# A two-layer graph network kernel: the bfloat16 split of layer two's rows moves into layer one's store

## The chip, the cores and the metric

The kernel runs on one NeuronCore of a Trainium2 chip. The metric is the time of one execution on the device in microseconds; the lower, the better. The profile is of one execution of the same program under the hardware profiler.

## The reference

50,000 nodes with 64 features each and 100,000 edges, sorted by destination (25,000 random ones, the same turned round, and one loop for each node). Two graph convolutions, a residual and a layer norm:

```
def _ngcf_conv(x, W1, W2, src, dst, n_nodes):
    deg_out = clip(segment_sum(ones, src), 1); deg_in = clip(segment_sum(ones, dst), 1)
    norm = rsqrt(deg_out[src] * deg_in[dst])
    msg = (x[src] @ W1 + x[src] * x[dst] @ W2) * norm[:, None]
    return x @ W1 + segment_sum(msg, dst)

h = relu(_ngcf_conv(x, W1_1, W2_1, src, dst, n))
h = _ngcf_conv(h, W1_2, W2_2, src, dst, n)
return _layernorm(x + h)              # float32, over the 64 features, eps 1e-5
```

## The kernel before

A node's message needs the sum S over its edges of the scaled source rows; then its result is (S + x) W1 + (S * x) W2, S scaled by the node's own factor. The kernel has a preparation (`prepare`: sort positions, degrees, factors, and layer one's table in HBM), layer one and layer two (`layer`, with l = 0 and l = 1), and behind them a general path that this input does not take.

Both layers have the same frame. The edges lie in 398 chunks of 128, gathered eight to a batch (51 batches, the last two of 4 and 2). The destinations are 392 tiles of 128 nodes, eight to a group (50 groups, the last two of 4). Step s of the loop in `STEPS` works on batch s. `ended(s)` names the groups whose last edges lie in batch s; nearly every step has one.

- GpSimd issues one indirect DMA for each chunk (line 799): 128 rows of the layer's table in HBM, one for each partition. In layer one the first 48 come from x itself (line 258). `rows` is a ring of 8 batches in layer one, 4 in layer two. A gather waits only until its slot is free: in layer one until the batch seven or eight back was cut (`rows_scaled`), in layer two until the batch four back was summed (`summed`).
- VectorE makes a batch's selection matrices (`select`, line 1077), one 0/1 matrix of 128 x up to 512 for a chunk.
- TensorE sums (`add_up`, line 828): for each chunk and each of up to four tiles three matmuls, one for each bfloat16 part of the gathered rows, whose sum is the float32 row to within rounding. The sums gather in PSUM (`p_sum`, three banks).
- Then a group goes through `join` (VectorE, adds the node's own row), `scale` (ScalarE), `products` (VectorE, S + x and S * x), `turn` (TensorE), `turned_back` (ScalarE), `multiply` (TensorE, line 853).
- In layer one ScalarE's `relu` makes the hidden rows and writes their first bfloat16 part into `y`; VectorE's `rests` (line 1114) writes what is left in float32 behind it, and SP stores the group to layer two's table (line 772). A row of that table is 384 bytes: 64 bfloat16 numbers and 64 float32 numbers. For the last four groups (`END_GROUPS`) VectorE does both in `end_rows` (lines 1154 and 1157).
- In layer two a group's end is the residual and the layer norm (`centre`, `square`, `vary`, `deviate`, `normalize`).

Where do the three parts come from? In layer one VectorE makes them of the gathered rows in `cut` (lines 1099, 1103, 1107): the scaled row `yr`, what is left behind its upper half, `rest`, and what is left behind that, `lo`. The upper half of a float32 number is read in place as a bfloat16 number, at a stride of two. In layer two the first part lies in the row, the second is the upper half of the float32 rest, and the third is made by VectorE in `last_part` (line 1087), which overwrites the rest's lower halves:

```
def last_part(b):
    left = first_and_rest(rows[:, b % RING, 0:BATCH[b]])[1]
    landed(dve, b)
    V.tensor_tensor(halves(left)[:, :, :, 0], left, halves(left)[:, :, :, 1], ALU.subtract).then_inc(split, 1)
```

`landed` waits for the batch's gathers. TensorE waits for `split` in both layers before it sums a batch.

Each engine works off its instructions in the order of the code. Some steps also make operands for a count of the edges (`hots`, lines 1121 and 1124; every second step of layer one from 8 to 44, three steps in four of layer two up to 41). In steps 0 to 4 of layer one VectorE looks up degrees (`pick`) between the instructions of `cut`. Layer two starts behind a barrier, once layer one's last store has landed.

Of the kernel before, what the change touches and what calls it, by code (L numbers as in the profile page):

```python
# [7 lines left out]
P = 128  # L8
# [583 lines left out]
GN = 8  # L592
# [36 lines left out]
def layer(nc, l, x, out, tables, flag, keepers):  # L629

    k = keepers
    with ExitStack() as ctx:
# [17 lines left out]
        if l == 0:  # L650
            rest, lo = sb("rest", [P, 2, 8, D]), sb("lo", [P, 2, 8, D], BF16)
# [3 lines left out]
            picks = sb("picks", [P, 2, TILES], F16)  # L655
# [4 lines left out]
            yr = sb("yr", [P, 2, 8, D])  # L660
# [17 lines left out]
        hots_made, counted, lanes_read, split = sem("hots_made"), sem("counted"), sem("lanes_read"), sem("split")  # L678
        if l == 0:
            rows_scaled, rest_made, hidden_made = (sem(n) for n in ("rows_scaled", "rest_made", "hidden_made"))  # L680
# [13 lines left out]
        def first_and_rest(a):  # L694

            return a.bitcast(BF16)[:, :, 0:D], a[:, :, D // 2:THREE]

        def halves(a):

            return a.bitcast(BF16).rearrange("p c (d two) -> p c d two", two=2)  # L700

        def parts(b):

            if l == 0:
                return tops(yr[:, b % 2]), tops(rest[:, b % 2]), lo[:, b % 2]
            first, left = first_and_rest(rows[:, b % RING])
            return first, halves(left)[:, :, :, 1], halves(left)[:, :, :, 0]
# [39 lines left out]
        def sync(sp):  # L747
# [14 lines left out]
            def store(g):  # L762
# [5 lines left out]
                if l == 0:  # L768
                    sp.wait_ge(high_made, g + 1)
                stores[g % 4] += 1  # L770
# [31 lines left out]
        def tensor(pe):  # L802
# [13 lines left out]
            def add_up(b):  # L816
                pe.wait_ge(sel_made, b + 1)
                pe.wait_ge(split, b + 1)
                for i in range(BATCH[b]):
# [4 lines left out]
                    for n, t in enumerate(band(c)):  # L824
                        g = GROUP_OF[t]
                        first = c == BEGINS[g] and t == GROUP[g][0]
                        for q, part in enumerate(parts(b)):
                            last = nc.tensor.matmul(p_sum[g % BANKS][:, t - GROUP[g][0], :], sel[:, b % 2, i, n * P:(n + 1) * P], part[:, i],  # L828
                                                    start=first and q == 0, stop=q == 2, skip_group_check=True)
# [12 lines left out]
            def multiply(g):  # L842
                pe.wait_ge(uvt_made, g + 1)
                if g in (g2, g3):
                    pe.wait_ge(uv_made, GROUPS)
                else:
                    done(pe, y_made if l == 0 else centred, g - 1)
# [50 lines left out]
        def scalar(act):  # L898
# [30 lines left out]
            def relu(g):  # L929
# [15 lines left out]
                A(first_and_rest(y[:, g % 4, 0:w])[0], from_rows, ACT.Copy).then_inc(high_made, 1)  # L945
# [31 lines left out]
            for s in STEPS:  # L977
# [11 lines left out]
                if l == 0:  # L989
                    for g in ended(s - 2):  # L990
                        relu(g)
# [42 lines left out]
        def vector(dve):  # L1034
# [48 lines left out]
            def last_part(b):  # L1083

                left = first_and_rest(rows[:, b % RING, 0:BATCH[b]])[1]
                landed(dve, b)
                V.tensor_tensor(halves(left)[:, :, :, 0], left, halves(left)[:, :, :, 1], ALU.subtract).then_inc(split, 1)  # L1087

            def cut(b):

                n, j = BATCH[b], b % 2
# [7 lines left out]
                V.tensor_tensor(yr[:, j, 0:n], rows[:, b % RING, 0:n, 0:D], rows[:, b % RING, 0:n, D:ROW].to_broadcast([P, n, D]), ALU.mult).then_inc(rows_scaled, 1)  # L1099
                pick_next(1)  # L1100
                dve.wait_ge(rows_scaled, b + 1)
                high = yr[:, j, 0:n].rearrange("p c d -> p (c d)")
                V.tensor_tensor(rest[:, j, 0:n].rearrange("p c d -> p (c d)"), high, top(high), ALU.subtract).then_inc(rest_made, 1)
                pick_next(2)
                dve.wait_ge(rest_made, b + 1)
                low = rest[:, j, 0:n].rearrange("p c d -> p (c d)")
                V.tensor_tensor(lo[:, j, 0:n].rearrange("p c d -> p (c d)"), low, top(low), ALU.subtract).then_inc(split, 1)
                pick_next(3)

            def rests(g):  # L1110

                dve.wait_ge(high_made, g + 1)
# [638 lines left out]
```

## Time and profile before

| | |
|---|---|
| time, median of 3 runs (lowest to highest) | 1152.91 us (1151.71 to 1153.17) |
| profiled execution, first to last instruction | 1700.1 us |
| busy in the profiled execution: TensorE, its weight loads | 1004.6 us, 885.6 us |
| VectorE | 998.9 us |
| ScalarE | 728.1 us |
| GpSimd | 831.9 us |
| mean granted TensorE clock | 0.727 |

The profiled execution has no other time of its own than this span, and the span is 547 us longer than a run. The profile's times of single instructions and their order can be read; its stretches can't be laid on a run's time as they stand. In the rows below a line gives the start in us from the first instruction, the duration in us, engine, line of the kernel, operation, what it writes and reads, the number of like instructions, and in square brackets how long the engine had been idle before it and what ended that. Instructions of one engine overlap by some 0.1 us, so that the distance from start to start is what one costs its engine. `issue` is time for which the profile shows no reason.

### The profile page before, as it was taken

The numbers are of one execution on the slowest core, as the hardware profiler recorded it, in microseconds if no ns is written. First come the engines' busy times: TensorE is split into PE (matmuls) and PEld (weight loads), VectorE is DVE, ScalarE is ACT, GpSimd is POOL, SyncE is SP. The second block draws the span as 40 slices with busy tenths as digits, with TensorE's granted clock in tenths as the row PEclk, the third lists the DMA queues.
The fourth block names the chain that finished last, engine by engine and source line by source line (L and its number), as shares of the span: only waits on it lengthen the run. The fifth ranks groups of instructions, "written<-read, shape, count | busy, mean of one in ns | idle before, by whom it ended". The sixth has DMA issues, their size and how long they took to land. (4 is left out here: it accounts for less than half of the span.)

```text
span 1700.1 us, 33320 instructions
## 1 busy us (share of the span) xinstructions
PE 1004.6 (59%) x13036; PEld 885.6 (52%) x13036; DVE 998.9 (59%) x2383; ACT 728.1 (43%) x2707; POOL 831.9 (49%) x819
## 2 busy tenths in 40 slices
PE   2661565656555655665488256667666666666656
PEld 1641354546445544554478135556665555556556
DVE  8992663445534543454378335666667666766557
ACT  3001133435534534453478103555444445554446
POOL 5786435533554455345510555555555555554550
PEclk9996566676766766676779567776777767777778
DMA  9861111111111111111111312322433332233322
GB/s 212 207 242 22 19 23 38 46 34 41 47 37 44 35 46 37 42 37 43 37 48 54 75 30 53 66 60 58 82 64 64 65 66 66 53 65 64 65 63 56
DMA packets 148697, 106.56 MB, mean 63 GB/s; under 512 B 115832, under 2 KB 128568, under 8 KB 147900
## 3 DMA queue, kind: packets, MB, share of 16 engines
q1 hardware_dynamic: 122856, 71.17, 15.5%
q0 software_dynamic: 25472, 32.83, 10.5%
q8 instruction: 103, 1.69, 0.4%
q10 hardware_dynamic: 212, 0.42, 0.1%
q14 instruction: 54, 0.44, 0.1%
HBM read 59.25 MB, written 45.11 MB: 61 GB/s over the span
## 5 line engine op out<-in xcount | busy, mean ns | idle before, releaser
L799 POOL DMA_INDIRECT c_rows<-table,k_row_i x398 | 386.5, 971 | 405.7 <-PE c_sum L828 226.1
L799 POOL DMA_INDIRECT k_rows<-table,k_row_i x350 | 344.9, 985 | 388.6 <-DVE c_yr L1099 289.0
L828 PE MATMUL c_sum<-c_rows,c_sel 128*128 128x64 bf16 x4665 | 265.5, 223 | 263.7 <-issue 241.9
L828 PEld LDWEIGHTS c_sum<-c_rows,c_sel 128*128 128x128 bf16 x4665 | 232.1, 118 | 296.1 <-issue 295.4
L926 ACT ACTIVATE c_uvt<-c_turn 128x512 f32<-128x512 f32 x196 | 106.4, 596 | 649.5 <-PE c_turn L860 606.5
L1136 DVE TENSOR_TENSOR c_sum<-c_sum,c_own 128x512 f32<-128x512 f32 x94 | 65.6, 698 | 473.2 <-PE c_sum L828 426.7
L853 PE MATMUL c_out<-k_wcat,c_uvt 128*128 128x64 f32 x1504 | 218.6, 307 | 77.9 <-ACT c_uvt L926 57.6
L828 PE MATMUL c_sum<-c_lo,c_sel 128*128 128x64 bf16 x1555 | 219.6, 218 | 71.8 <-issue 71.7
L828 PE MATMUL c_sum<-c_yr,c_sel 128*128 128x64 bf16 x1555 | 220.9, 218 | 68.6 <-issue 67.9
L853 PEld LDWEIGHTS c_out<-k_wcat,c_uvt 128*128 128x128 f32 x1504 | 206.5, 219 | 101.1 <-ACT c_uvt L926 74.7
L828 PE MATMUL c_sum<-c_rest,c_sel 128*128 128x64 bf16 x1555 | 220.1, 218 | 64.1 <-issue 64.0
L1077 DVE TENSOR_SCALAR c_sel<-k_place,k_grid 128x512 bf16<-128x512 f16 (+2 forms) x796 | 230.6, 358 | 23.7 <-PE c_sum L828 23.7
L828 PEld LDWEIGHTS c_sum<-c_lo,c_sel 128*128 128x128 bf16 x1555 | 173.2, 114 | 84.5 <-issue 84.3
L828 PEld LDWEIGHTS c_sum<-c_yr,c_sel 128*128 128x128 bf16 x1555 | 177.3, 117 | 74.2 <-issue 74.1
L828 PEld LDWEIGHTS c_sum<-c_rest,c_sel 128*128 128x128 bf16 x1555 | 174.3, 115 | 78.2 <-issue 77.8
L918 ACT ACTIVATE c_sum<-c_sum,k_xh 128x64 f32<-128x64 f32 x752 | 162.2, 317 | 77.3 <-DVE c_sum L1136 77.1
L905 ACT ACTIVATE c_own<-k_xh 128x64 f32<-128x64 f32 x752 | 193.6, 399 | 0.0
L860 PE MATMUL c_turn<-k_ident,c_uv 128*128 128x128 f32 x784 | 145.0, 344 | 3.7 <-issue 3.6
L860 PEld LDWEIGHTS c_turn<-k_ident,c_uv 128*128 128x128 f32 x784 | 119.5, 183 | 5.2 <-issue 4.8
L1171 DVE TENSOR_TENSOR c_uv<-c_sum,k_xh 128x512 f32<-128x512 f32 (+1 forms) x100 | 67.6, 676 | 80.6 <-ACT c_sum L918 45.1
L1124 DVE TENSOR_SCALAR c_hot_t<-k_place,k_grid 128x392 f16<-128x392 f16 x398 | 102.0, 327 | 0.0
L258 POOL DMA_INDIRECT k_rows<-in_x,k_row_i x48 | 78.0, 1626 | 38.5 <-DVE k_row_i L498 24.2
(210 smaller groups left out, 1247.8 us busy)
## 6 DMA issues: line engine op xcount, KB each, us to landing
table<-c_y SPq DMA_DIRECT2D x48, 384.0 KB, 2.3
out<-c_y SPq DMA_DIRECT2D x48, 256.0 KB
c_res<-in_x SPq DMA_DIRECT2D x46, 256.0 KB
c_rows<-table,k_row_i POOLq DMA_INDIRECT x398
k_rows<-table,k_row_i POOLq DMA_INDIRECT x350
table<-k_xh SPq DMA_DIRECT2D x1, 3640.0 KB
table<-k_xh SPq DMA_DIRECT2D x2, 1820.0 KB
table<-k_xh SPq DMA_DIRECT2D x1, 3542.5 KB
```

Of the source, the lines that this page charges most:

```text
L258: G.indirect_dma_start(out=k.rows[:, c // 8, c % 8, 0:D], out_offset=None, in_=x, in_offset=bass.IndirectOffsetOnAxis(ap=k.row_i[:, c:c + ...
L799: nc.gpsimd.indirect_dma_start(out=rows[:, b % RING, i], out_offset=None, in_=tables[l], in_offset=bass.IndirectOffsetOnAxis(ap=k.row_i[:, ...
L828: last = nc.tensor.matmul(p_sum[g % BANKS][:, t - GROUP[g][0], :], sel[:, b % 2, i, n * P:(n + 1) * P], part[:, i], start=first and q == 0 ...
L853: last = nc.tensor.matmul(out_bank(g)[:, n, :], uvt[:, g % 2, n, :], weights, start=True, stop=True)
L860: last = nc.tensor.transpose(turn_bank(g, n)[:, n % 4, :], uv[:, g % 2, n].rearrange("p a d -> p (a d)"), k.ident[:, :])
L905: last = A(own[:, g % 2, t - a, :], k.xh[:, t, 0:D], ACT.Copy, scale=k.xh[:, t, D:ROW])
L918: last = A(p_sum[g % BANKS][:, t - a, :], p_sum[g % BANKS][:, t - a, :], ACT.Copy, scale=k.xh[:, t, D:ROW])
L926: last = A(uvt[:, g % 2, h:h + 4, :], turn_bank(g, h)[:, :, :], ACT.Copy)
L1077: last = V.tensor_scalar(sel[:, b % 2, i, 0:w], k.place[:, a:a + w], k.grid[:, 2, BACK + c:BACK + c + 1], None, ALU.is_equal)
L1124: last = V.tensor_scalar(hot_t[:, m], k.place[:, 0:TILES], k.grid[:, 0, slot], None, ALU.is_equal)
L1136: V.tensor_tensor(bank[:, 0:w], bank[:, 0:w], own_rows, ALU.add).then_inc(sums_made, 1)
L1171: V.tensor_tensor(uv[:, j, 0:w, 0, :], bank[:, 0:w], h, ALU.add)
```

## The change

A row of layer two's table now holds three bfloat16 parts, 64 numbers each, again 384 bytes. Layer one makes all three before the store: `relu` the first on ScalarE as before, `rests` the remainder in float32 into a buffer of its own, `left` (one for all groups), then the new `middles` on ScalarE copies the remainder's upper half as the second part, and the new `lows` on VectorE subtracts it from the remainder and writes the third. `left` may be written again once `middles` of the group before has read it. SP's store waits for all three. TensorE's `multiply` in layer one waits for `left_made` where it waited for `y_made`.

In layer two `last_part` is gone, and TensorE waits for the landing of the gathers itself. In layer one `yr`, `rest` and `lo` become three planes of one buffer, `cuts`, and the third part is written at a stride of two like the others are read. `picks` lies in a part of `y` that is not yet in use.

```
-            for q, part in enumerate(parts(b)):
-                ... part[:, i] ...
+            for q in range(3):
+                ... parts(b, i)[:, q] ...
 def add_up(b):
     pe.wait_ge(sel_made, b + 1)
-    pe.wait_ge(split, b + 1)
+    if l == 0:
+        pe.wait_ge(split, b + 1)
+    else:
+        landed(pe, b)
 ...
+def middles(g):
+    act.wait_ge(left_made, g + 1)
+    A(part(y[:, g % 4, 0:wide(g)], 1), upper(left[:, 0:wide(g)]), ACT.Copy).then_inc(middle_made, 1)
 ...                                   # scalar, in each step of layer one
+                    for g in ended(s - 3):
+                        middles(g)
                     for g in ended(s - 2):
                         relu(g)
 ...                                   # scalar, end of layer one
+                middles(g0 - 2)
                 relu(g0 - 1)
                 turned_back(g0)
                 turned_back(g1)
+                middles(g0 - 1)
                 turned_back(g2)
                 turned_back(g3)
                 for g in END_GROUPS:
                     relu(g)
+                    middles(g)
                     hidden_end(g)
 ...
-def last_part(b):
-    left = first_and_rest(rows[:, b % RING, 0:BATCH[b]])[1]
-    landed(dve, b)
-    V.tensor_tensor(halves(left)[:, :, :, 0], left, halves(left)[:, :, :, 1], ALU.subtract).then_inc(split, 1)
 def cut(b):
-    V.tensor_tensor(yr[...], rows[...], factors, ALU.mult).then_inc(rows_scaled, 1)
-    V.tensor_tensor(rest[...], high, top(high), ALU.subtract).then_inc(rest_made, 1)
-    V.tensor_tensor(lo[...], low, top(low), ALU.subtract).then_inc(split, 1)
+    V.tensor_tensor(high, rows[...], factors, ALU.mult).then_inc(rows_scaled, 1)
+    V.tensor_tensor(rest, high, upper(high), ALU.subtract).then_inc(rest_made, 1)
+    V.tensor_tensor(upper(low), rest, upper(rest), ALU.subtract).then_inc(split, 1)
 def rests(g):
     dve.wait_ge(high_made, g + 1)
-    V.tensor_tensor(left, p_out[g % 2][:, 0:wide(g)], first, ALU.subtract).then_inc(y_made, 1)
+    done(dve, middle_made, g)
+    V.tensor_tensor(left[:, 0:w], p_out[g % 2][:, 0:w], part(y[:, g % 4, 0:w], 0), ALU.subtract).then_inc(left_made, 1)
+def lows(g):
+    rest = left[:, 0:wide(g)]
+    dve.wait_ge(left_made, g + 1)
+    V.tensor_tensor(part(y[:, g % 4, 0:wide(g)], 2), rest, upper(rest), ALU.subtract).then_inc(y_made, 1)
 ...                                   # vector, each step: products(ended(s - 1)), then
+                if l == 0:
+                    for g in ended(s - 3):
+                        lows(g)
```

What it moves, in the order of each engine's instructions. VectorE at the end of layer one, the four end groups; `c_hot_t` is the scaled hidden row, `c_left` the remainder, `c_y` the row to be stored. Before:

```order
L1154 SCALAR_TENSOR_TENSOR c_hot_t<-c_out,k_xh 128x512
L1157 TENSOR_TENSOR c_y<-c_hot_t 128x8x64
L1154 SCALAR_TENSOR_TENSOR c_hot_t<-c_out,k_xh 128x512
L1157 TENSOR_TENSOR c_y<-c_hot_t 128x8x64
L1154 SCALAR_TENSOR_TENSOR c_hot_t<-c_sum,k_xh 128x256
L1157 TENSOR_TENSOR c_y<-c_hot_t 128x4x64
```

The same place now:

```order
L1165 SCALAR_TENSOR_TENSOR c_hot_t<-c_out,k_xh 128x512
L1168 TENSOR_TENSOR c_left<-c_hot_t 128x512
L1125 TENSOR_TENSOR c_y<-c_left 128x8x64
L1165 SCALAR_TENSOR_TENSOR c_hot_t<-c_out,k_xh 128x512
L1168 TENSOR_TENSOR c_left<-c_hot_t 128x512
L1125 TENSOR_TENSOR c_y<-c_left 128x8x64
L1165 SCALAR_TENSOR_TENSOR c_hot_t<-c_sum,k_xh 128x256
```

Each group has three instructions in place of two.

VectorE at the end of layer two, from the selection of the last but one batch to the join of group g1; `c_rows` are the gathered rows, `c_sel` the selection matrices. Before:

```order
L1087 TENSOR_TENSOR c_rows<-c_rows 128x4x64
L1077 TENSOR_SCALAR c_sel<-k_place,k_grid 128x512 x2
L1202 TENSOR_TENSOR c_out<-c_res,c_out 128x512
L1204 TENSOR_REDUCE c_total<-c_out 128x8
L1206 SCALAR_TENSOR_TENSOR c_z<-c_total,c_out 128x512
L1087 TENSOR_TENSOR c_rows<-c_rows 128x2x64
L1136 TENSOR_TENSOR c_sum<-c_sum,c_own_end 128x512
L1145 TENSOR_TENSOR c_sum<-c_sum,k_xh 128x512
```

Now:

```order
L1088 TENSOR_SCALAR c_sel<-k_place,k_grid 128x512 x2
L1215 TENSOR_TENSOR c_out<-c_res,c_out 128x512
L1217 TENSOR_REDUCE c_total<-c_out 128x8
L1219 SCALAR_TENSOR_TENSOR c_z<-c_total,c_out 128x512
L1147 TENSOR_TENSOR c_sum<-c_sum,c_own_end 128x512
L1156 TENSOR_TENSOR c_sum<-c_sum,k_xh 128x512
```

The two instructions on `c_rows`, which waited for the last landings, are gone, and the rest closes up.

ScalarE in a middle step of layer one, from `add_own` to `turned_back`. Before:

```order
L905 ACTIVATE c_own<-k_xh 128x64 x8
L937 ACTIVATE k_xh<-c_out 128x8x64
L940 ACTIVATE c_out<-c_out,k_xh 128x64 x8
L945 ACTIVATE c_y<-c_out 128x8x64
L926 ACTIVATE c_uvt<-c_turn 128x512 x2
```

Now:

```order
L907 ACTIVATE c_own<-k_xh 128x64 x8
L951 ACTIVATE c_y<-c_left 128x8x64
L939 ACTIVATE k_xh<-c_out 128x8x64
L942 ACTIVATE c_out<-c_out,k_xh 128x64 x8
L947 ACTIVATE c_y<-c_out 128x8x64
L928 ACTIVATE c_uvt<-c_turn 128x512 x2
```

The copy of the second part of an older group stands ahead of `relu`.

## Rows read from the trace of the kernel before

**Rows 1.** The page's first line.
```profile
span 1700.1 us, 33320 instructions
```
**Rows 2.** Waits in total: engine, waiting line, releaser; us, times, longest.
```profile
PE c_sum L828 <- issue: 445.5, 524, 2.6
```
**Rows 3.** Order of time, TensorE in a batch of layer two.
```profile
1365.79 0.21 PE L828 MATMUL c_sum<-c_rows,c_sel 128*128 128x64 bf16 x1 [1.20 <-issue]
...
1370.08 3.31 PE L828 MATMUL c_sum<-c_rows,c_sel 128*128 128x64 bf16 x59 [1.20 <-issue]
```
**Rows 4.** Order of time, first gathers of layer two and the first last_part.
```profile
956.37 0.95 POOL L799 DMA_INDIRECT c_rows<-table,k_row_i  x1 [0.30 <-issue]
957.62 0.94 POOL L799 DMA_INDIRECT c_rows<-table,k_row_i  x1 [0.30 <-issue]
957.64 0.73 DVE L1087 TENSOR_TENSOR c_rows<-c_rows 128x512 bf16<-128x512 f32 x1 [9.70 <-DMA c_rows<-table,k_row_i]
```
**Rows 5.** Order of time, first gather of the table in layer one, in layer two.
```profile
140.74 0.94 POOL L799 DMA_INDIRECT k_rows<-table,k_row_i  x1 [0.30 <-issue]
...
946.33 0.98 POOL L799 DMA_INDIRECT c_rows<-table,k_row_i  x1 [72.45 <-POOLq L1671]
```
**Rows 6.** Order of time, VectorE at the end of layer one.
```profile
929.28 0.28 DVE L1099 TENSOR_TENSOR c_yr<-k_rows 128x128 f32<-128x128 f32 x1
...
939.93 0.42 DVE L1154 SCALAR_TENSOR_TENSOR c_hot_t<-c_sum,k_xh 128x256 f32<-128x256 f32 x1 [0.81 <-PE c_sum L853]
...
941.34 0.42 DVE L1157 TENSOR_TENSOR c_y<-c_hot_t 128x256 f32<-128x256 f32 x1
```
**Rows 7.** Order of time, VectorE at the end of layer two.
```profile
1664.55 0.72 DVE L1087 TENSOR_TENSOR c_rows<-c_rows 128x512 bf16<-128x512 f32 x1
...
1671.72 0.73 DVE L1087 TENSOR_TENSOR c_rows<-c_rows 128x512 bf16<-128x512 f32 x1
1672.34 0.70 DVE L1136 TENSOR_TENSOR c_sum<-c_sum,c_own 128x512 f32<-128x512 f32 x1
...
1678.23 0.42 DVE L1087 TENSOR_TENSOR c_rows<-c_rows 128x256 bf16<-128x256 f32 x1
...
1681.13 0.29 DVE L1087 TENSOR_TENSOR c_rows<-c_rows 128x128 bf16<-128x128 f32 x1
```
**Rows 8.** Groups from 159 to 254 us: busy, mean ns, idle before by releaser.
```profile
L799 POOL DMA_INDIRECT k_rows<-table,k_row_i x43 | 41.0, 955 | 55.9 <-DVE c_yr L1099 44.6 <-issue 11.3
```
**Rows 9.** Order of time, three starts of cut in layer one, without pauses.
```profile
881.29 0.68 DVE L1099 TENSOR_TENSOR c_yr<-k_rows 128x512 f32<-128x512 f32 x1
...
887.84 0.68 DVE L1099 TENSOR_TENSOR c_yr<-k_rows 128x512 f32<-128x512 f32 x1
...
896.97 0.68 DVE L1099 TENSOR_TENSOR c_yr<-k_rows 128x512 f32<-128x512 f32 x1
```
**Rows 10.** Window of layer two: length, busy (x) by engine, clock, DMA share, GB/s.
```profile
1103.00:1591.00 488.00, 318.96 (x4080) 285.61 (x4081) 320.48 (x787) 241.53 (x940) 257.19 (x264) 0.73 0.31 65
```
**Rows 11.** Order of time, ScalarE in a step of layer one, without pauses.
```profile
884.07 1.72 ACT L918 ACTIVATE c_sum<-c_sum,k_xh 128x64 f32<-128x64 f32 x8 [0.16 <-DVE c_sum L1136]
...
889.98 0.60 ACT L945 ACTIVATE c_y<-c_out 128x512 bf16<-128x512 f32 x1
...
891.43 1.74 ACT L918 ACTIVATE c_sum<-c_sum,k_xh 128x64 f32<-128x64 f32 x8
```
**Rows 12.** Groups of the whole trace: TensorE's sum on yr and on lo.
```profile
L828 PE MATMUL c_sum<-c_yr,c_sel 128*128 128x64 bf16 x1555 | 220.9, 218 | 68.6 <-issue 67.9 <-DVE c_lo L1107 0.2
L828 PE MATMUL c_sum<-c_lo,c_sel 128*128 128x64 bf16 x1555 | 219.6, 218 | 71.8 <-issue 71.7
```
**Rows 13.** Order of time, last_part and gathers that were issued in it.
```profile
1205.18 0.71 DVE L1087 TENSOR_TENSOR c_rows<-c_rows 128x512 bf16<-128x512 f32 x1
1205.24 1.44 POOL L799 DMA_INDIRECT c_rows<-table,k_row_i  x1 [0.30 <-issue]
...
1665.00 1.05 POOL L799 DMA_INDIRECT c_rows<-table,k_row_i  x1 [0.30 <-issue]
```

More of the change, by code:

```diff
@@ L692, in layer, with upper, part, parts @@
         out_full = out[0:FULL_TILES * P, :].rearrange("(t p) d -> p t d", p=P)
[L694 to L702, printed above, removed]
+        def upper(a):
+            return a.bitcast(BF16).rearrange("p c (d two) -> p c d two", two=2)[:, :, :, 1]
+        def part(a, q):
+            return a.bitcast(BF16)[:, :, q * D:(q + 1) * D]
+        def parts(b, i):
             if l == 0:
-                return tops(yr[:, b % 2]), tops(rest[:, b % 2]), lo[:, b % 2]
-            first, left = first_and_rest(rows[:, b % RING])
-            return first, halves(left)[:, :, :, 1], halves(left)[:, :, :, 0]
+                return upper(cuts[:, b % 2, i])
+            return rows[:, b % RING, i].bitcast(BF16).rearrange("p (q d) -> p q d", q=3)
         STEPS = range(BATCHES - 3)
@@ L769, in store @@
                     sp.wait_ge(high_made, g + 1)
+                    sp.wait_ge(middle_made, g + 1)
                 stores[g % 4] += 1
@@ L826, in add_up @@
                         first = c == BEGINS[g] and t == GROUP[g][0]
-                        for q, part in enumerate(parts(b)):
-                            last = nc.tensor.matmul(p_sum[g % BANKS][:, t - GROUP[g][0], :], sel[:, b % 2, i, n * P:(n + 1) * P], part[:, i],
+                        for q in range(3):
+                            last = nc.tensor.matmul(p_sum[g % BANKS][:, t - GROUP[g][0], :], sel[:, b % 2, i, n * P:(n + 1) * P], parts(b, i)[:, q],
                                                     start=first and q == 0, stop=q == 2, skip_group_check=True)
@@ L846, in multiply @@
                 else:
-                    done(pe, y_made if l == 0 else centred, g - 1)
+                    done(pe, left_made if l == 0 else centred, g - 1)
                 weights = k.wcat[:, l, :]
@@ L1081, in select @@
                         pick(LOOKUPS[b - 1], 4 + i // 2)
[L1083 to L1087 removed]
             def cut(b):
[L1091 removed]
+                n = BATCH[b]
+                high, rest, low = (cuts[:, b % 2, 0:n, q, :] for q in range(3))
                 def pick_next(i):
@@ L1155, in end_rows @@
                 dve.wait_ge(flat_made, g + 1)
+                done(dve, middle_made, g)
+                V.tensor_tensor(left[:, 0:w], flat[:, j, 0:w], tops(flat[:, j, 0:w]), ALU.subtract).then_inc(left_made, 1)
                 done(dve, stored[g % 4], 16 * (g // 4))
-                V.tensor_tensor(first_and_rest(y[:, g % 4, 0:w])[1], flat[:, j, 0:w], tops(flat[:, j, 0:w]), ALU.subtract).then_inc(y_made, 1)
+                lows(g)
             def normalize(g):
@@ L1260, in vector @@
             select(0)
-            split_up = (cut, last_part)[l]
             for s in STEPS:
-                split_up(s)
+                if l == 0:
+                    cut(s)
                 for g in ended(s - 1):
@@ L1276, in vector @@
                     products(g)
+                if l == 0:
+                    for g in ended(s - 3):
+                        lows(g)
                 if l == 0 and s == 10:
@@ L1294, in vector @@
                         verdict()
-            split_up(b0)
+            if l == 0:
+                cut(b0)
             join(g0)
@@ L1303, in vector @@
             if l == 0:
+                lows(g0 - 2)
                 cut(b1)
@@ L1310, in vector @@
                 products(g1)
+                lows(g0 - 1)
             else:
```

22 lines of the change are left out of this document (8 added, 14 removed).

## The prediction

> **What bounds the kernel now.** I read the page's first lines, then the waits, because span and run disagree: the profiled execution takes 1700.1 us from first to last instruction [rows 1], a run without the profiler 1152.91 (median). There is no longer time to put around that span; the extra 547 us lie inside it. The waits show them: TensorE's sum, line 828, waits 445.5 us on "issue" [rows 2]. In the order of time these are matmuls that stand alone, each behind up to 1.2 us of "issue", in the middle of a batch, and then 59 in 3.31 us [rows 3]. Nothing in the program makes such a pause, so I take it for one of the profiled execution and leave it out. Between 875 and 930 us it is absent; there the steps of layer one follow each other as fast as the engines allow.
>
> Which engine, then, bounds a run? While nothing holds it, the GpSimd queue issues a gather every 1.25 us (956.37 to 957.62 [rows 4]). At that spacing the 350 gathers that layer one issues itself take 437.5 us and the 398 of layer two 497.5. Around them I put: the first one of layer one at 140.7 [rows 5]; from the end of its last one to layer two's first, 1.6 us for the landing (956.37 + 0.95 to 957.64 [rows 4]) and 17.0 from the last batch's cut at 929.28 [rows 6] to 946.33 [rows 5]; and behind the last gather of all 1.6 to 3.2 (the landing, then VectorE's turn) and 19.0 from 1681.13 [rows 7] to 1700.1. Sum: 140.7 + 437.5 + 18.6 + 497.5 + 21 to 22 = about 1115. In the first five steps GpSimd also waits 44.6 us for the cut [rows 8], of which a part may come from the profiler: 1115 to 1160. The measured 1152.9 lies between. So the gathers are the path nearly everywhere, and at most 38 us are left for everything else.
>
> VectorE is next. Without pauses a step of layer one takes it 6.55 us (881.29 to 887.84), and 9.13 (887.84 to 896.97) where it also makes the counting operands [rows 9], against 8 x 1.25 = 10.0 for a batch of gathers. Layer two, steps 9 to 41: 320.48 us of VectorE beside 264 gathers, which are 33 batches [rows 10]: 9.7 each. A gather waits only for the sum four batches back, so a single long step of VectorE costs GpSimd nothing; the mean counts.
>
> **The change, part by part.** (a) In layer two last_part goes: 51 instructions of line 1087, a full one 0.62 us from its start to the next (1671.72 to 1672.34 [rows 7]), some 31 us of VectorE. GpSimd's issue hides it: with 9.7 under 10.0 it is worth nothing; with that cover gone, up to 31 us. I take 0, the row of 9.7 being the nearer one. TensorE now waits for the landing itself, and VectorE no longer stands behind it.
>
> (b) Layer two's end, where VectorE is paced by itself. The last parts there are 0.62, and 0.42 and 0.29 less the 0.1 of overlap that the first shows [rows 7], together 1.1 us; and joins, products and centring of older groups are no longer queued behind a landing. Bounds -1.1 and -3; I take -1.9.
>
> (c) Layer one, steady: one subtraction more a group (lows), 0.6 us as last_part takes [rows 7], and one ScalarE copy, 0.60 us like line 945's [rows 11]. VectorE's steps become 7.2 and 9.7, under 10.0; ScalarE, busy without a gap for 7.4 us a step (884.07 to 891.43 [rows 11]), goes to 7.9. Both hide behind the gathers: 0; uncovered it would be 44 x 0.6 = 26. The store is issued some 4 us later; its buffer comes round after four groups, 40 us. The moved waits don't grow: TensorE's multiply waits for the first subtraction, which stands where it did, and middles(g) stands on ScalarE behind scale, whose own wait (the join) lies just ahead of rests on VectorE. TensorE's reads change their stride, but a matmul on the contiguous lo and one on the strided yr both take 218 ns [rows 12]: 0.
>
> (d) The first steps of layer one, where GpSimd waits for the cut [rows 8]: lows of groups 0 and 1 fall in steps 4 and 5. 0 to +1.2; I take +0.9.
>
> (e) Layer one's end, which delays layer two's first gather. Two lows of whole groups ahead of the last sums, 1.2 us, and one in each end group, 0.6 + 0.6 + 0.4 + 0.4 (the small ones like the 0.42 at 941.34 [rows 6]), of which VectorE's wait of 0.81 at 939.93 [rows 6] takes back 0.8: +2.4. Lowest +1.2 (only the last two groups count), highest +3.2.
>
> (f) A cost that the engines' sums don't show. A gather issued while VectorE subtracts one SBUF tensor from another lasts longer: line 1087 at 1205.18 for 0.71, the gather at 1205.24 for 1.44 instead of 0.94 [rows 13]. The one issued at 957.62, 0.02 ahead of such an instruction, keeps 0.94 [rows 4]. Of 21 instructions of line 1087 that ran beside a gather seven had started ahead of it, and the excess of those gathers summed to 2.2 us (the last, at 1665.00, is 1.05 long [rows 13]). So an instruction of this kind costs GpSimd 2.2 / 21 = 0.10 us, and with GpSimd as the bound that is time. Layer two loses 51 of them, layer one gains about 44 while gathers run: -5.3 + 4.6 = -0.7. Each side is, by 0 to 0.31 an instruction, between -15.8 and 0, and between 0 and +13.6.
>
> The Trainium skill ("SBUF — State Buffer", section "Who interferes with whom") says that a DVE instruction with two SBUF inputs contends with a GpSimd instruction that reads SBUF. By that rule, the trace agrees: 1.44 against 0.94. The same section infers that a tensor_tensor does not hold up a GpSimd DMA's descriptors; by that (f) would be 0 and the sum 0.7 us higher. Here the trace differs.
>
> Sum: -1.9 + 0.9 + 2.4 - 0.7 = +0.7. Every term stands for an execution without the pauses, so it is set on the median and not on the span: 1153.6 us.
>
> **The rivals.** R1, VectorE bounds layer two. For it: a step without counting operands takes VectorE 7.2 us (1664.55 to 1671.72 [rows 7]), so that three in four with them take (4 x 9.7 - 7.2) / 3 = 10.5, over 10.0; and up to 38 us of the run are unexplained. Against it: the mean is 9.7, and only the mean counts. If waits inside the steps bring layer two to 10.4 a step or more, the change wins what lies over the gathers' 10.0, 0.4 us in each of 40 steps, 16 us: 1138.
>
> R2, on the other side: lows stands at a fixed distance behind the landing and so in a fixed place of the gathers' beat. If that is just ahead of an issue, all 44 hit, at the 0.31 of the seven seen: +13.6. And layer two may have nothing to give back, since line 1087, when it waits for its landing, starts 0.02 us behind an issue (957.62, 957.64 [rows 4]), the place that costs nothing. 1152.9 - 1.9 + 0.9 + 2.4 + 13.6 = 1168. It decides from 0.02 us per lows above what layer two saves. Against it: the landing wanders, and VectorE's way to lows is not always the same.
>
> R3, the change doesn't do what it says: VectorE leaves last_part and waits as long for TensorE's sum at the join, and the ends cancel: 1153.
>
> **How the numbers follow.** Forecast 0.52, R1 0.24, R2 0.17, R3 0.07. A measurement of this kernel tells 0.2%, 2.3 us, from no change. The forecast's own range, with both sides of (f) half open, is 1147 to 1160; of its 0.52 some 0.15 lie below 1150.6, 0.22 within, 0.15 above 1155.2. So faster 0.15 + 0.24 = 0.39, same 0.22 + 0.07 = 0.29, slower 0.15 + 0.17 = 0.32. The range takes in R1 and the lower part of R2: 1137 to 1163.
>
> **What would show it.** In the profile after, with the same pauses: in layer two no VectorE instruction that writes c_rows and none that a DMA releases at a step's start; between the pauses a layer-one step of 7.2 us instead of 6.55; from the last cut of layer one to layer two's first gather 2.4 us more than 17.0; gathers still 1.25 us apart, some long ones beside lows in layer one and fewer in layer two. The forecast is wrong if a run gains over 6 us (then VectorE bounded layer two, R1) or loses over 7 (R2: many gathers of 1.2 to 1.4 us beside lows).

## The result, and the profile after

The changed kernel took 1159.87 us (median of 20 runs, 1156.64 to 1166.97), the kernel before 1155.65 (20 runs, 1151.34 to 1159.88). The ratio on record is 1.0043, with a 95% interval from 1.0026 to 1.0059: slower, by more than the 0.2% that can be told. (The quotient of the two medians is 1.0037; for all runs below the ratio on record and this quotient lie within 0.15% of each other.) In the sets at some 1155 us single runs of one kernel lie up to 15 us apart, and the median of before moved from 1152.7 to 1159.7 between sets of runs, so only ratios within one set are compared below. In one set every kernel, before too, took some 1725 us, with matmuls that stand apart as in [rows 3].

The profiled execution of after (its run took 1161.82 us) has none of the pauses of [rows 2]. From its page: the span, the busy times, the chain of waits by engine, and the two groups of gathers (busy, mean ns of one | idle before them, and why).

```profile
span 1160.2 us, 33419 instructions
PE 837.8 (72%) x13036; PEld 781.6 (67%) x13036; DVE 1001.9 (86%) x2382; ACT 752.6 (65%) x2757; POOL 846.2 (73%) x819
POOL 33%; issue 11%; DVE 1%; PE 1%; DMA 0%; POOLq 0%; ACT 0%; DVEq 0%; ACTq 0%
L798 POOL DMA_INDIRECT c_rows<-table,k_row_i x398 | 384.9, 967 | 143.3 <-issue 121.1
L798 POOL DMA_INDIRECT k_rows<-table,k_row_i x350 | 360.8, 1031 | 106.7 <-issue 106.7
```

The same lines of an execution of before that also has no pauses (first experiment; it is the fastest of that experiment's 12 runs, 1152.35 us at a median of 1159.21):

```profile
span 1150.7 us, 33320 instructions
PE 818.2 (71%) x13036; PEld 756.2 (66%) x13036; DVE 996.9 (87%) x2383; ACT 728.6 (63%) x2707; POOL 838.3 (73%) x819
POOL 33%; issue 11%; DVE 1%; ACT 0%; DMA 0%; POOLq 0%; DVEq 0%; ACTq 0%
L799 POOL DMA_INDIRECT c_rows<-table,k_row_i x398 | 384.6, 966 | 142.9 <-issue 121.0
L799 POOL DMA_INDIRECT k_rows<-table,k_row_i x350 | 353.2, 1009 | 106.7 <-issue 106.4
```

In both, GpSimd never waits for another engine inside a layer: 106.7 us of "issue" before 350 gathers is 0.30 a piece, the gap of [rows 4]. The 44.6 us of [rows 8] are gone with the pauses. So a run is a sum of five pieces: the time to the first gather, the stretch of layer one's 350 gathers, the gap to layer two's first, the stretch of its 398, and the tail. In us, each piece from the start of one gather to the start of another; "held back" is the sum of what the gathers last over 0.944, their usual duration, from the trace's unrounded times:

| execution | first gather | layer one (held back) | gap | layer two (held back) | tail | span |
|---|---|---|---|---|---|---|
| before, 1152.35 | 140.73 | 458.64 (22.8) | 22.83 | 504.63 (8.9) | 23.87 | 1150.7 |
| after, 1161.82 | 140.73 | 466.25 (30.4) | 23.19 | 505.08 (9.2) | 24.95 | 1160.2 |
| after, last set, 1155.72 | 140.75 | 463.48 (27.6) | 23.88 | 501.17 (5.4) | 24.82 | 1154.1 |

Most of the 9.5 us between the first two is layer one's stretch, 7.6 us, and that is its held-back time, 7.6 us more. But one execution each doesn't show what the change costs there: in the second experiment layer one is unchanged, and its one trace, of its slowest run, has a stretch of 464.10 us with 28.3 held back. The busy time of VectorE, 5 us more, and of ScalarE, 24 more, are in no piece. What holds a gather back stands in the order of time of after, VectorE first (line 1125 is lows; lines 1184 and 1185 are the products), then the gathers (start, duration):

```profile
304.61 0.68 DVE L1184 TENSOR_TENSOR c_uv<-c_sum,k_xh 128x512 f32<-128x512 f32 x1
305.20 0.68 DVE L1185 TENSOR_TENSOR c_uv<-c_sum,k_xh 128x512 f32<-128x512 f32 x1
305.80 0.68 DVE L1125 TENSOR_TENSOR c_y<-c_left 128x512 bf16<-128x512 f32 x1
306.40 0.68 DVE L1132 TENSOR_TENSOR c_hot_l<-k_lanes,c_lane 128x1024 f16<-128x1024 f16 x1
```
```profile
304.62 0.94 POOL L798 DMA_INDIRECT k_rows<-table,k_row_i  x1 [0.30 <-issue]
305.87 1.43 POOL L798 DMA_INDIRECT k_rows<-table,k_row_i  x1 [0.30 <-issue]
307.60 0.94 POOL L798 DMA_INDIRECT k_rows<-table,k_row_i  x1 [0.30 <-issue]
```

A gather that starts 0.07 us into lows lasts 1.43, as one in last_part did in [rows 13]. Sorting all 350 gathers of layer one by the VectorE instruction that was running at their start (the last one to have started), 24 began in a lows and were held back 10.4 us in sum, 0.43 each; in the last set 25, 11.1 us. The kernel before shows both kinds side by side. In its trace without pauses 70 gathers of layer one began in one of the cut's three instructions, which have both operands in SBUF, and were held back 19.9 us; 51 began in a product (lines 1171 and 1172), which has one operand in PSUM, and were held back 0.05 us.

In layer two VectorE no longer waits for the landing, and waits for the sum and ScalarE instead. Totals of its waits (us, times, longest), after, then before without pauses:

```profile
DVE c_sum L1147 <- PE c_sum L830: 42.4, 20, 6.0
DVE c_uv L1184 <- ACT c_sum L920: 31.7, 32, 1.4
PE c_sum L830 <- DMA c_rows<-table,k_row_i: 107.6, 42, 18.1
```
```profile
DVE c_rows L1087 <- DMA c_rows<-table,k_row_i: 63.7, 32, 9.6
```

### The profile page after: what moved, and what is told of

Same layout as the page of the kernel before. It is cut to its first block and busy times, and to the rows that moved or that the text cites. A ratio compares the mean times of both kernels' runs of the same rounds, so it can differ in the third digit from the quotient of the medians.

```text
span 1160.2 us, 33419 instructions
## 1 busy us (share of the span) xinstructions
PE 837.8 (72%) x13036; PEld 781.6 (67%) x13036; DVE 1001.9 (86%) x2382; ACT 752.6 (65%) x2757; POOL 846.2 (73%) x819
## 3 DMA queue, kind: packets, MB, share of 16 engines
q1 hardware_dynamic: 122856, 71.17, 22.8%
## 5 line engine op out<-in xcount | busy, mean ns | idle before, releaser
L798 POOL DMA_INDIRECT k_rows<-table,k_row_i x350 | 360.8, 1031 | 106.7 <-issue 106.7
L830 PE MATMUL c_sum<-c_rows,c_sel 128*128 128x64 bf16 x4665 | 202.7, 218 | 117.7 <-DMA c_rows<-table,k_row_i 107.6
L830 PEld LDWEIGHTS c_sum<-c_rows,c_sel 128*128 128x128 bf16 x4665 | 197.4, 115 | 123.6 <-issue 110.0
L830 PEld LDWEIGHTS c_sum<-c_cuts,c_sel 128*128 128x128 bf16 x4665 | 186.4, 109 | 7.1 <-issue 6.7
L830 PE MATMUL c_sum<-c_cuts,c_sel 128*128 128x64 bf16 x4665 | 186.3, 208 | 3.9 <-DVE c_cuts L1111 3.9
L862 PE MATMUL c_turn<-k_ident,c_uv 128*128 128x128 f32 x784 | 108.6, 283 | 10.6 <-DVE c_uv L1185 10.6
L1147 DVE TENSOR_TENSOR c_sum<-c_sum,c_own 128x512 f32<-128x512 f32 x94 | 65.7, 698 | 44.0 <-PE c_sum L830 42.4
L862 PEld LDWEIGHTS c_turn<-k_ident,c_uv 128*128 128x128 f32 x784 | 88.4, 147 | 12.4 <-DVE c_uv L1185 12.4
L1184 DVE TENSOR_TENSOR c_uv<-c_sum,k_xh 128x512 f32<-128x512 f32 (+1 forms) x100 | 66.5, 665 | 31.8 <-ACT c_sum L920 31.7
L971 ACT ACTIVATE c_y<-c_z,c_rstd 128x64 f32<-128x64 f32 x360 | 91.6, 368 | 0.3 <-DVE c_rstd L1229 0.3
L840 PE MATMUL k_p_count<-c_hot_t,c_hot_l 128*128 128x392 f16 x398 | 75.4, 332 | 7.8 <-DVE c_hot_t L1135 7.7
L942 ACT ACTIVATE c_out<-c_out,k_xh 128x64 f32<-128x64 f32 x368 | 79.3, 304 | 1.5
L299 PE MATMUL a_bank<-a_spreads,a_hot 128*128 128x28 f16 x784 | 50.5, 226 | 32.3 <-DVE a_hot L448 25.4
## 6 DMA issues: line engine op xcount, KB each, us to landing
table<-k_xh SPq DMA_DIRECT2D x1, 3542.5 KB, 10.8
```

The lines of the kernel that those rows point to most:

```text
L798: nc.gpsimd.indirect_dma_start(out=rows[:, b % RING, i], out_offset=None, in_=tables[l], in_offset=bass.IndirectOffsetOnAxis(ap=k.row_i[:, ...
L862: last = nc.tensor.transpose(turn_bank(g, n)[:, n % 4, :], uv[:, g % 2, n].rearrange("p a d -> p (a d)"), k.ident[:, :])
L942: last = A(bank[:, t - a, :], bank[:, t - a, :], ACT.Relu, scale=k.xh[:, t, D:ROW])
L971: last = A(y[:, g % 4, n, :], z[:, g % 4, n, :], ACT.Copy, scale=rstd[:, g % 4, n:n + 1])
```

## The experiments

Two theories stood against each other. **L**: gathers are the path, and a VectorE instruction with two SBUF operands that runs when one starts holds it back. **E**: the loss is at the layers' ends, and the gathers' stretches are equal. A third, that VectorE's own time counts, joined them later.

**1. Before again.**

> The kernel before, profiled once more, to have a trace of it without the pauses of the first one. Theory L (gathers are the path, and a subtraction of two SBUF tensors that is running when a gather is issued holds it back): time 1155, every gather in layer one and two back to back; layer one's 350 gathers about 6 to 10 us quicker from first to last than the 466 us of the changed kernel, because the 24 hits of lows (10 us) are missing; in layer two line 1087 hits some gathers. Theory E (the loss lies at the ends of the layers and the gathers' stretches are equal): both stretches within 1 us of the changed kernel's 466 and 505, and 4 us less between them.

Measured: 1159.21 us (12 runs), 0.9999 times before (0.9977 to 1.0021). Its trace is the first row of the table: inside the layers no gather waits for another engine, so the 38 us that the prediction left "for everything else" are 22.8 and 8.9 us of gathers held back, a longer gap and a longer tail. Layer one's stretch is 7.6 us shorter than after's, as L has it, but it comes from before's fastest run.

**2. Layer two's half alone.** The kernel before without last_part; TensorE waits for the landing, and its third matmul reads the second part once more, so the kernel leaves out the third part.

```
-  split_up = (cut, last_part)[l]
-  pe.wait_ge(split, b + 1)
+  if l == 0: pe.wait_ge(split, b + 1)
+  else: landed(pe, b)
```

> The kernel before with only the layer-two half of the change: no last_part, TensorE waits for the landing. It leaves the third part out (the third matmul reads the second part again). L: the saving is the hits of line 1087 on gathers plus the end of layer two: 2 to 7 us less than before, 1149 to 1153. E: only the end, 1 to 2 us, 1154. If VectorE bounded layer two: 10 us or more less.

Measured: 1151.15 us (8 runs), 0.9914 (0.9881 to 0.9948). The medians are 8.5 us apart, more than either theory had (2 to 7 us, 1 to 2 us). The one trace of it is of its slowest run (1158.28) and shows no gain where the edit lies: layer two's stretch is 504.83 us, held back 9.2, against 504.63 and 8.9. So the gain is measured and its place isn't.

**3. Layer one's half alone.** The changed kernel with an instruction like last_part kept in layer two (third part plus zero, in place, TensorE waits for it).

```
+  third = part(rows[:, b % RING, 0:BATCH[b]], 2)
+  V.tensor_tensor(third, third, <zeros>, ALU.add).then_inc(split, 1)
```

> The changed kernel with a last_part kept in layer two: a VectorE instruction with two SBUF inputs of the same size and place (the third part plus zero), for which TensorE waits. So only the layer-one half of the change is left. L: changed kernel plus what e2 saved: 1162 to 1166. E: 1161 to 1162.

Measured: 1160.16 us (12 runs), 0.9995 (0.9972 to 1.0017). In its trace 26 gathers began in lows, 10.8 us in sum, and layer one's stretch is 461.82 us. Both theories expected at least 1161 us, although before was 4 us slower here than they assumed; that miss has no explanation. The two halves give -0.9% and 0.0%, the whole +0.4%: they don't add up. The changed kernel wasn't in this set, so the three were never compared side by side.

**4. The remainder stays in PSUM.** Outside the end groups the first subtraction writes its PSUM bank in place, and lows subtracts the middle part from PSUM, so that only one of its operands is in SBUF. The multiplication waits for lows, since the bank is busy longer, and lows waits for ScalarE's middles.

```
-  V.tensor_tensor(left[:, 0:w], p_out[g % 2][:, 0:w], part(y[:, g % 4, 0:w], 0), ALU.subtract)
+  V.tensor_tensor(p_out[g % 2][:, 0:w], p_out[g % 2][:, 0:w], part(y[:, g % 4, 0:w], 0), ALU.subtract)
-  V.tensor_tensor(part(y[:, g % 4, 0:w], 2), left, upper(left), ALU.subtract)
+  V.tensor_tensor(part(y[:, g % 4, 0:w], 2), p_out[g % 2][:, 0:w], part(y[:, g % 4, 0:w], 1), ALU.subtract)
```

> The changed kernel, but outside of the last four groups the remainder stays in the PSUM bank that holds the row, so that neither of the two subtractions has two SBUF inputs; as many instructions of the same sizes as in the changed kernel. L: no gather is held back by lows; layer one's gathers about 10 us quicker, 1148 to 1152, faster than the kernel before by what layer two saves. E: as the changed kernel, 1159 to 1161, since VectorE's and ScalarE's work is the same.

Measured: 1150.43 us (8 runs), 0.9911 (0.9882 to 0.9940): faster than before beside it (after wasn't in this set). Layer one's stretch fell to 452.66 us, held back 16.8; 22 gathers began in lows and none was held back. The gap grew to 31.18 us. Its profiled run is only 1.7 us faster than before's, because before's is its fastest, so the traces don't place the whole 0.9%.

**5 to 8. A set at 1725 us.** After again; before with one more subtraction a group at the place of lows, once with two SBUF operands and once with one in PSUM; and the fourth kernel with a mended end (shown under the eleventh run). The result of the added subtraction is read by nobody, but the next multiplication waits for it in both.

```
+  def more(g):
+      first, left = first_and_rest(y[:, g % 4, 0:wide(g)])
+      dve.wait_ge(y_made, g + 1)
+      V.tensor_tensor(spare[:, 0:wide(g)], left, halves(left)[:, :, :, 1], ALU.subtract)   # two in SBUF
+      V.tensor_tensor(spare[:, 0:wide(g)], p_out[g % 2][:, 0:wide(g)], first, ALU.subtract)   # or this: one in PSUM
```

> The changed kernel again, beside the three others of this set and on the same chip, since medians of sets taken at other times differ by some 4 us for one kernel. Theory L (the gathers are the path; a VectorE subtraction with two SBUF operands that is running when a gather starts holds it back): 1.000 to 1.006 times before, and in the profiled run again some 25 gathers of layer one held back by the rests' last subtraction, 9 to 12 us in sum, and a stretch of layer-one gathers of 463 to 468 us. Theory E (the loss lies at the layers' ends): the same ratio, but the stretches of gathers as long as before's (459 and 505 us) and the gap from layer one's last gather to layer two's first over 24 us.

> The kernel before with one more VectorE subtraction for each group of layer one (43 groups outside the end), put where the changed kernel forms its third part: rest less its upper half, both operands in SBUF, the result to a spare buffer that nobody reads; the group's multiplication waits for it. Theory L: some 24 of the 43 are running when a gather starts and cost about 0.43 us each, so the stretch of layer-one gathers grows by about 10 us over before's and the kernel takes 1.005 to 1.010 times before. A theory by which only VectorE's own time counts (43 instructions of 0.6 to 0.7 us, 28 us of work) expects the same here as of the run with the operand in PSUM. Theory E: both within 0.2% of before, since neither touches the ends.

> The same extra subtraction at the same place, with the same waits and the same spare result, but its first operand is the group's bank in PSUM (the hidden rows) and its second the first part in SBUF. Theory L: no gather is held back by it, and the kernel takes 0.998 to 1.002 times before, 0.5 to 1.0% less than the run with both operands in SBUF. The theory that VectorE's own time counts: no difference between the two runs.

> The changed kernel with the remainder left in PSUM, as in the run of the set before, except for the last group before the end groups, whose remainder goes to the SBUF buffer again, so that VectorE's last subtraction of that group need not wait for ScalarE (3.08 us of wait at 609.47 us there, and a gap of 31.2 us from layer one's last gather to layer two's first, where the changed kernel has 23.2). Theory L: the short stretch of layer-one gathers stays (451 to 456 us) and the gap falls to 23 to 25 us, so 6 to 8 us less than 1150.43 beside its own runs of before: 0.984 to 0.988 times before. If the gap stays at 31 us, the wait was not what made it, and the ratio stays at 0.991.

Measured, before at 1725.12 us (29 runs): after 1.0043 (1.0015 to 1.0072), two SBUF operands 1.0069 (1.0046 to 1.0092), one in PSUM 1.0057 (1.0030 to 1.0084), PSUM and end 1.0219 (1.0186 to 1.0252). Here GpSimd does wait; the waits in total of after in this set:

```profile
PE c_sum L830 <- issue: 472.5, 550, 2.6
POOL k_rows L798 <- DVE c_cuts L1105: 298.0, 26, 15.8
POOL c_rows L798 <- PE c_sum L830: 238.3, 47, 6.1
```

TensorE's chain sets the time, with gathers waiting 298 and 238 us, so there is room to hide a gather held back, and the two extra subtractions cannot be told apart: this set doesn't test L. Against the expectations, the subtraction with one operand in PSUM wasn't free here, and PSUM and end is far from its 0.984 to 0.988. The set shows that the same kernels rank otherwise when another engine is the path. The PSUM version is the slowest here. Layer one's stretch of gathers is 771 us against 744 of after; TensorE waits for its transposed operand 49 us in it against 32, which fits a multiplication that waits for a bank, but no run took that wait alone.

**9 and 10. The pair again, with the gathers as the path.**

> The kernel before with the extra subtraction of two SBUF operands once more: in the set before, every kernel (before too) took some 1725 us, with matmuls far apart, and the gathers waited for TensorE, so a gather held back could cost nothing there. This run is one where the gathers are the path, if before takes some 1155 us again. Theory L: the stretch of layer-one gathers about 10 us longer than before's 459, 1.005 to 1.010 times before. The theory that VectorE's own time counts: as the run with the operand in PSUM. Theory E: within 0.2% of before.

> The kernel before with the extra subtraction of one PSUM and one SBUF operand once more, beside the run with two SBUF operands. Theory L: no gather held back by it, 0.998 to 1.002 times before, 0.5 to 1.0% less than the run with two SBUF operands. The theory that VectorE's own time counts: both runs alike. (In the set at 1725 us they were alike: 1.0069 and 1.0057 times before.)

Measured, before at 1152.81 us (23 runs): two SBUF operands 1158.05 us, 1.0041 (1.0021 to 1.0062); one in PSUM 1150.74 us, 0.9980 (0.9959 to 1.0001), 12 runs each. The ratio with two in SBUF is a little under L's 1.005 to 1.010. The groups of the added instruction (x, busy, mean ns) are alike, first two SBUF operands, then one in PSUM:

```profile
L1121 DVE TENSOR_TENSOR c_spare<-c_y 128x512 bf16<-128x512 f32 x46 | 31.2, 679 | 0.0
```
```profile
L1121 DVE TENSOR_TENSOR c_spare<-c_out,c_y 128x512 bf16<-128x512 f32 x46 | 31.1, 677 | 0.0
```

Same place, same 31 us, same waits. In the order of time a gather starts 0.06 us into each. Two SBUF operands:

```profile
311.94 0.68 DVE L1121 TENSOR_TENSOR c_spare<-c_y 128x512 bf16<-128x512 f32 x1
...
312.00 1.43 POOL L800 DMA_INDIRECT k_rows<-table,k_row_i  x1 [0.30 <-issue]
313.74 1.03 POOL L800 DMA_INDIRECT k_rows<-table,k_row_i  x1 [0.30 <-issue]
```

One in PSUM:

```profile
303.31 0.68 DVE L1121 TENSOR_TENSOR c_spare<-c_out,c_y 128x512 bf16<-128x512 f32 x1
...
303.37 0.94 POOL L800 DMA_INDIRECT k_rows<-table,k_row_i  x1 [0.30 <-issue]
304.62 1.01 POOL L800 DMA_INDIRECT k_rows<-table,k_row_i  x1 [0.30 <-issue]
```

22 gathers began in the one, of which 20 were held back, 9.1 us in sum; 23 began in the other and none was. Layer one's stretches are 461.0 and 456.3 us: 4.7 apart and not 9.1, since the cut's three instructions hold gathers back 10.9 us in the first and 17.2 in the second. L had expected a stretch some 10 us over before's 459; it is 2 us over that one trace. So the mechanism is L's and the net size is smaller. VectorE's 31 us cost nothing, the operands 0.6% between the two runs. The theory that VectorE's own time counts falls. E doesn't fit either: here 0.6% comes from instructions inside the layer, with gaps of 20.9 and 19.7 us, and in the table gap and tail together grow by only 1.4 and 2.0 us.

The edit moves one operand to PSUM and also changes the second, from the upper halves at a stride of two to the first part without gaps. The stride isn't what holds a gather back: the multiplication of line 1099 in before reads no upper halves, and 25 gathers that began in it were held back 7.6 us.

**11 and 12. PSUM with its end mended, and after beside it.** The last group before the end groups puts its remainder in SBUF again, and so doesn't wait for ScalarE's middles.

```
-  rest = (left if g in END_GROUPS else p_out[g % 2])[:, 0:wide(g)]
+  rest = (left if g >= g0 - 1 else p_out[g % 2])[:, 0:wide(g)]
```

> The changed kernel with the remainder in PSUM except for the last group before the end groups, once more, where the gathers are the path (before at some 1155 us; in the set at 1725 us it was the slowest, 1.0219 times before, because there TensorE's chain set the time and the multiplication waits longer for its bank). Theory L: a stretch of layer-one gathers of 451 to 456 us and a gap of 23 to 25 us from layer one's last gather to layer two's first, 0.984 to 0.988 times before. If the gap stays at 31 us, the wait of VectorE's last subtraction was not what made it, and the ratio is 0.991.

> The changed kernel beside it on the same chip. Both theories: 1.002 to 1.008 times before. Theory L: a stretch of layer-one gathers 8 to 15 us longer than in the kernel beside it, with 20 to 28 of the gathers held back by the rests' last subtraction for 8 to 12 us in sum, and a gap within 1 us of the other's.

Measured, before at 1152.71 us (19 runs): after 1157.40 us, 1.0039 (1.0014 to 1.0064), 12 runs; PSUM and end 1145.68 us, 0.9930 (0.9903 to 0.9956), 8 runs. Against after that is 1.1% less by the ratios, and layer one's stretch is 13 us shorter than after's, with profiled runs close to their medians. But the ratio is not the 0.984 to 0.988 of theory L, and the extra 0.5% that the mended end was to bring isn't there: the interval holds the fourth kernel's ratio. Layer one's stretch is 450.43 us, 27 gathers began in lows and none was held back, and the gap fell only from 31.2 to 27.6 us, where 23 to 25 was expected. Its gathers and VectorE at the end of layer one (line 1106 is the last batch's cut):

```profile
591.20 1.09 POOL L798 DMA_INDIRECT k_rows<-table,k_row_i  x1 [0.30 <-issue]
618.84 0.98 POOL L798 DMA_INDIRECT c_rows<-table,k_row_i  x1 [26.54 <-POOLq L1694]
```
```profile
591.51 0.69 DVE L1109 TENSOR_TENSOR c_cuts<-c_cuts 128x512 f32<-128x512 f32 x1
...
599.77 0.28 DVE L1106 TENSOR_TENSOR c_cuts<-k_rows 128x128 f32<-128x128 f32 x1
...
611.67 0.69 DVE L1174 TENSOR_TENSOR c_left<-c_hot_t 128x512 f32<-128x512 f32 x1 [1.59 <-ACT c_y L952]
```

The last gather ends at 592.29, but its cut starts 7.5 us later and without a wait, where it comes 2.6 us behind the gather in before and after. Between 200 and 590 us no cut waits for a landing in this kernel; that stretch's largest wait of VectorE is the first row below (us, times, longest), a lows waiting for ScalarE's middles; those of before and after are the two others:

```profile
DVE c_y L1129 <- ACT c_y L952: 15.3, 34, 2.1
```
```profile
DVE c_yr L1099 <- DMA k_rows<-table,k_row_i: 43.4, 18, 4.3
```
```profile
DVE c_cuts L1105 <- DMA k_rows<-table,k_row_i: 19.0, 9, 3.6
```

So, by this trace, VectorE no longer keeps up once its gathers aren't held back: it reaches the end of layer one late, with its own work and these 15.3 us of waits, and what the mended end gives is lost. That is read from the trace; no run took VectorE's work or its waits away.

## Why the prediction came out as it did

The forecast was 1153.6 us, 0.7 over before; the loss measured in the two sets where the gathers are the path is 4.2 and 4.7 us between medians, 0.43 and 0.39% by the ratios. (The set at 1725 us has 0.43% too, but another engine as the path.) The range, 26 us wide, holds the time; the sum had the right sign by cancelling terms that are partly wrong, which is luck, and the chances leant to faster (0.39) over slower (0.32), and slower came. What bounds the kernel was read rightly: gathers nearly everywhere, at 1.25 us, and VectorE and ScalarE with room beside them. By its steps:

**The pauses** of [rows 2, 3] were put down to the profiled execution. That is wrong as stated: in the set at 1725 us all runs are that long, and the profiled executions of the other sets have none. That they play no part in a run of 1153 us holds. The 44.6 us of [rows 8] belong to them too.

**(a)** holds as far as the traces show: no gather of layer two waits for another engine in before, so last_part's 37 us of VectorE bound nothing by their length. As R3 had it, VectorE waits for the sum and ScalarE in place of the landing, 42.4 and 31.7 us in the whole of after.

**(b)** -1.9 us, isn't seen: the tail is 23.87 us in before and 24.95 and 24.82 in after. In the executions of the other kernels without pauses it lies between 21.8 and 26.6, so a gain of 1.1 could hide in that spread, but no trace points to one.

**(c)** 0, holds: the pair of runs shows 31 us of VectorE at that very place costing nothing by its time. The ScalarE copies were not tried alone; their 24 us are in no piece of the table.

**(d)** +0.9 falls: without pauses GpSimd doesn't wait in the first steps, so nothing could be delayed.

**(e)** +2.4, measured +0.35 to +0.9. From the last cut to layer two's first gather, before has 622.20 - 602.90 = 19.30 us, after 630.17 - 610.52 = 19.65, and 20.18 in the last set. VectorE's waits there, before, then after:

```profile
606.50 0.69 DVE L1114 TENSOR_TENSOR c_y<-c_out,c_y 128x512 f32<-128x512 f32 x1 [1.31 <-ACT c_y L945]
...
613.58 0.69 DVE L1154 SCALAR_TENSOR_TENSOR c_hot_t<-c_out,k_xh 128x512 f32<-128x512 f32 x1 [0.95 <-PE c_out L853]
...
615.81 0.42 DVE L1154 SCALAR_TENSOR_TENSOR c_hot_t<-c_sum,k_xh 128x256 f32<-128x256 f32 x1 [0.81 <-PE c_sum L853]
...
621.63 0.09 DVE L1255 MEMSET c_std<- 128x32 f32 x1 [3.99 <-PEq L1671]
```
```profile
613.26 0.69 DVE L1119 TENSOR_TENSOR c_left<-c_out,c_y 128x512 f32<-128x512 f32 x1 [0.45 <-ACT c_y L947]
...
623.01 0.69 DVE L1168 TENSOR_TENSOR c_left<-c_hot_t 128x512 f32<-128x512 f32 x1 [1.63 <-ACT c_y L951]
...
629.61 0.09 DVE L1268 MEMSET c_std<- 128x32 f32 x1 [2.46 <-PEq L1688]
```

The lows went into waits that before had: 1.31 + 0.95 + 0.81 + 3.99 = 7.1 us of them against 0.45 + 1.63 + 2.46 = 4.5. The prediction took back one of the four. (The wait of 1.63, for the single buffer of the rests, is the change's own.)

**(f)** had the mechanism, and both its terms had the wrong size. Layer one, +4.6: 24 of the group subtractions meet a gather at 0.43 us, 10.4 us, 0.24 an instruction in place of 0.10. They are not all net: the cut's three instructions, moved by lows, hold gathers back 14.0 us in after against 19.9 in before. Net held back in layer one against that one execution of before: 7.6 us in one execution of after, 4.8 in the other. Against the second experiment's 28.3, of its slowest run, it would be 2.1 and -0.7, so the net size is known only roughly; the ratio of the ninth to the tenth run, 0.6%, is the firmer figure. Layer two, -5.3: last_part held gathers back 3.1, 3.5 and 1.5 us in the three executions that have it as before does, 0.05 an instruction, and without it the counting operand of line 1132, also with two SBUF operands, meets more of them: 4.3 and 3.4 us against 1.0, 1.0 and 0.5. So layer two's gathers give back nothing that the traces show, though the second experiment's 0.9% says that something was gained. The step that failed is the one that took a rate per instruction from last_part and used it for lows. The rate belongs to a place in the gathers' beat. R2 said so, with "a fixed distance behind the landing", and was right in kind: about half of the groups meet a gather instead of all. The 10.4 us lie nearer to its 13.6 than to the 4.6 of the sum. (By the whole trace the prediction's own count is 19 instructions and 2.1 us, not 21 and 2.2; the rate comes out near 0.11 all the same.)

The Trainium skill ("SBUF — State Buffer", section "Who interferes with whom") says that a DVE instruction with at most one SBUF input, outside the modes that use both ports, does not contend with GpSimd. By that rule, the runs agree: 1.43 us against 0.94 in the ninth and tenth. Where it infers that a tensor_tensor leaves a GpSimd DMA's descriptors alone, the traces differ: 1.43 us in the ninth run as in [rows 13].

**R1**, VectorE as the bound of layer two, doesn't fit the traces: in before, without pauses, no gather of layer two waits for it, and the whole change gained nothing. The second experiment's 0.9% is of the size that R1 would give, and stays unexplained. Something like R1 is seen in layer one of the eleventh run, where VectorE falls behind.

## What to carry to other kernels

When one engine issues DMAs all through a kernel and is the path, another engine's instruction beside it isn't priced by its length but by whether it delays an issue: look for an issue whose duration is longer than its fellows', and at what ran when it started. On VectorE, putting one of two operands in PSUM made an instruction of the same length free here. It also holds the bank longer; the kernel that does so was 2% slower than before where TensorE was the path, and whether for that reason is not shown. A rate measured for one instruction doesn't carry to another at a different place of the beat, and halves of a change are only comparable with the whole when all are in the same set of runs.

## What the runs showed of the hardware

A gather that starts in a VectorE instruction with two SBUF operands mostly ends some 0.82 us behind it (306.48 + 0.82 in the rows above; 312.62 + 0.81 in the ninth run), so the earlier its start in it, the more it loses, up to some 0.5 us. The very start is free: in before, of the gathers that begin in the cut's instructions, those 0.03 us in keep 0.94 us, and those from 0.05 us in last up to 1.46. A comparison with one tensor operand can do it too, rarely: this gather of layer two in after started in one of line 1135.

```profile
703.21 1.67 POOL L798 DMA_INDIRECT c_rows<-table,k_row_i  x1 [0.30 <-issue]
```

Three of the 43 that did so in that layer last 1.66 us or more, the others 1.09 at most. The three began 0.39 us behind the first comparison of their row of eight, but in the last set gathers at that place last 0.97, so what tells them apart stays open. So does the gain of layer two's half alone (second experiment), for which no trace of a typical run exists, and why its 0.9% is not in the whole.

The landing of a batch comes 2.6 us behind the end of its last gather at layer one's end (607.92 to 610.52 in after, 600.31 to 602.90 in before), not the 1.6 us that the prediction took from layer two's start. (Its 1.6 runs from the end of the batch's eighth gather, 955.12 + 0.95, to 957.64; the gather whose numbers it gives is the ninth, and ended only 0.32 us ahead.)
